# Routing's exponentials ahead of the gelus, route products ahead of an output projection, late normalisations and transposes earlier among the shared experts

## What is computed

```python
x = x + xattn(layernorm(x), ctx, ctx, Wq, Wk, Wv, Wo)   # 16 heads of 8, softmax over the HEADS (axis=1)
x = x + ffn(layernorm(x))

def ffn(x):                       # 8 routed experts, 2 shared ones, F = 512
    raw = x @ centroids.T
    routing_scores = sigmoid(raw); balanced = sigmoid(raw + routing_bias)
    _, top_idx = top_k(balanced, 2)
    top_w = softmax(take(routing_scores, top_idx))
    shared_out = sum over 2 shared experts of gelu(x @ Wfc.T) @ Wproj.T
    routed_out = sum over the 2 chosen experts of top_w * (gelu(x @ Wfc.T) @ Wproj.T)
    return x + shared_out + routed_out
```

## Time and profile before

| | |
|---|---|
| median of three runs | 400.84 us (398.72 to 401.91) |
| the profiled execution | 401.8 us, its span 399.9 us |
| TensorE busy | 319.1 us, 80% of the span |
| VectorE, ScalarE, GpSimd busy | 270.1, 250.5, 258.7 us |
| chain that ended last, by engine | TensorE 31%, issue 24%, VectorE 23%, GpSimd 11% |

### The profile page before, as it was taken

The page is one execution under the profiler, slowest core; times in us unless marked ns, Lnnn a source line. Parts: engine busy times, 40 slices in busy tenths (PEclk is TensorE's granted clock), DMA queues, the critical chain, the costliest instruction groups (busy, mean ns, idle before and its releaser), DMA issues.

```text
span 399.9 us, 11184 instructions
## 1 busy us (share of the span) xinstructions
PE 319.1 (80%) x3828; PEld 258.4 (65%) x3829; DVE 270.1 (68%) x570; ACT 250.5 (63%) x464; POOL 258.7 (65%) x268
## 2 busy tenths in 40 slices
PE   4865786577667687999999999799999999999100
PEld 1562464444444465888788888699898989999100
DVE  3789999989999976652774000367676667676167
ACT  2778798586786762756434355366676776767075
POOL 6344779789787692777777771057777777777500
PEclk9999899988988998999999999999999999999755
DMA  8956343400000000111113612213232232232097
GB/s 255 334 149 246 105 134 112 126 3 2 2 2 2 2 2 7 51 52 55 55 40 96 130 48 75 53 41 88 82 93 83 69 91 74 78 84 62 8 366 259
DMA packets 29176, 36.12 MB, mean 90 GB/s; under 512 B 4932, under 2 KB 24007, under 8 KB 28624
## 3 DMA queue, kind: packets, MB, share of 16 engines
q1 hardware_dynamic: 24592, 27.13, 22.0%
q0 software_dynamic: 4544, 8.44, 6.7%
HBM read 21.74 MB, written 14.72 MB: 91 GB/s over the span
## 4 chain that ended last, share of the span: by engine, by line
PE 31%; issue 24%; DVE 23%; POOL 11%; ACT 5%; DMA 4%; POOLq 1%; SPq 1%; DVEq 1%; ACTq 0%
PE banks L1410 13%; POOL results L502 11%; DVE Z L885 6%; DVE Mx L880 3%; PE banks L1396 3%; PE banks L1395 3%; PE banks L1394 3%; DVE X L1176 2%; DVE rZ L888 1%; ACT E L626 1%; DVE X L1182 1%; DVE stats L856 1%; PE banks L1279 1%; DMA q_rows<-qRep 1%; DMA qRep<-results 1%
## 5 line engine op out<-in xcount | busy, mean ns | idle before, releaser
L502 POOL DMA_INDIRECT results<-E,qRep x78 | 85.9, 1101 | 49.6 <-issue 27.6
L484 POOL DMA_INDIRECT gathered<-xs,slot x64 | 63.4, 991 | 27.6 <-issue 18.6
L430 POOL TENSOR_TENSOR E<-E,rZ 128x1024 f32<-128x1024 f32 x32 | 67.4, 2130 | 18.6 <-DVE rZ L888 18.6
L1147 DVE TENSOR_TENSOR E<-hid,E 128x512 f16<-128x512 f32 x78 | 54.0, 692 | 36.2 <-ACT E L753 36.2
L751 ACT ACTIVATE hid<-banks 128x512 f32<-128x512 f32 x78 | 47.0, 602 | 39.3 <-DVE E L1147 21.8
L1492 PE MATMUL banks<-wprojL,E 128*128 x312 | 54.6, 219 | 2.8 <-DVE E L1147 1.8
L1496 PE MATMUL banks<-wprojH,E 128*128 x312 | 54.3, 219 | 0.0
L1494 PE MATMUL banks<-wprojH,E 128*128 x312 | 54.3, 219 | 0.0
L753 ACT ACTIVATE E<-banks 128x512 f16<-128x512 f32 x78 | 47.3, 606 | 0.0
L626 ACT ACTIVATE E<-banks 128x1024 f32<-128x1024 f32 x32 | 33.2, 1095 | 20.4 <-PE banks L1279 20.4
L1478 PE MATMUL banks<-qRep,wfcH 128*128 128x256 f16 x156 | 42.6, 273 | 0.8 <-ACT E L753 0.6
(11 more groups left out here) (203 smaller groups left out, 726.1 us busy)
## 6 DMA issues: line engine op xcount, KB each, us to landing
qRep<-gathered SPq DMA_DIRECT2D x39, 129.0 KB
qRep<-q_rows SPq DMA_DIRECT2D x32, 128.0 KB, 2.5
qRep<-results SPq DMA_DIRECT2D x8, 512.0 KB, 7.3
X<-in_x SPq DMA_DIRECT2D x4, 512.0 KB, 6.2
q_rows<-qRep SPq DMA_DIRECT2D x8, 256.0 KB, 2.1
out<-X SPq DMA_DIRECT2D x8, 256.0 KB, 4.0
results<-E,qRep POOLq DMA_INDIRECT x78, 2.5
gathered<-spare SPq DMA_DIRECT2D x9, 129.0 KB, 3.9
```

The lines of the kernel that those rows point to most:

```text
L430: g.tensor_tensor(heads, heads, rZ[:, k % 2, :].unsqueeze(1).unsqueeze(3).broadcast_to([P, HH // 2, P, 2]), ALU.mult).then_inc(attn_ready, 1)
L484: g.indirect_dma_start(out=gathered, out_offset=bass.IndirectOffsetOnAxis(ap=slot[:, k, i:i + 1], axis=0), in_=xs[:, i, :], in_offset=None ...
L502: g.indirect_dma_start(out=results, out_offset=bass.IndirectOffsetOnAxis(ap=xg[:, k, h, 2 * D:ROW].bitcast(I32), axis=0), in_=yg[:, k, h, ...
L1147: v.tensor_tensor(gL[:, j, 2 * c:2 * c + 2], hid[:, 2 * j + c].rearrange("p (c q) -> p c q", c=2), gH[:, j, 2 * c:2 * c + 2], ALU.subtract ...
```

## The change

TensorE: the projection of unit 13 moves from ahead of the first up products to behind `route(0)`. Transposes of pair 4 move from behind expert 1 into it (after its second step), those of pair 5 from behind expert 2 to behind expert 1, pair 6 from behind expert 3 to behind expert 2, pair 7 from expert 4 (third step) to expert 3 (second step). `route(1)` moves from behind expert 4 to behind expert 3, `ranks(1)` from the first step of expert 6 to the third step of expert 5. ScalarE: `sigmoid_exps(0)` moves ahead of the four gelus of expert 0 (it stood behind them and behind `copy_o` of unit 14), `copy_o` of unit 14 stands behind the first of these gelus and not the fourth, the normalisations of pairs 4 and 5 stand behind the first and second gelu of expert 1 (both stood ahead of its fourth), the copies of the transposes and `sigmoid_exps(1)` move with TensorE's order. VectorE and GpSimd are untouched, and no instruction is added or taken away but table loads.

```diff
--- before.py
+++ after.py
@@ -706,32 +706,35 @@
                 act.wait_ge(rneed, 2 * portion + 2)
                 s.activation(rt[:, 1:3, lo:hi], rt[:, 1:3, lo:hi], ACT.Exp, scale=-1.0).then_inc(rexp, 1)
 
-            gelus(0, 0, False)
+            sigmoid_exps(0)
+            gelu(0, 0, 0, False)
             act.wait_ge(y_ready, UNITS - 3)
             copy_o(UNITS - 2, 0)
-            sigmoid_exps(0)
+            for c in range(1, FC):
+                gelu(0, 0, c, False)
             act.wait_ge(y_ready, UNITS - 2)
             copy_o(UNITS - 1, 1)
             for c in range(FC):
+                gelu(1, 1, c, False)
+                if c < 2:
+                    second_norm(PAIRS // 2 - 2, c, True)
+            for c in range(FC):
+                if c == 1:
+                    copy_x2(LATE)
                 if c == FC - 1:
-                    for j in range(2):
-                        second_norm(PAIRS // 2 - 2, j, True)
-                gelu(1, 1, c, False)
-            for i in range(2, 4):
-                for c in range(FC):
-                    if c == FC - 1:
-                        copy_x2(LATE + i - 2)
-                    gelu(i, i % 2, c, True)
+                    copy_x2(LATE + 1)
+                gelu(2, 0, c, True)
             for c in range(FC):
                 if c == FC - 1:
                     copy_x2(PAIRS - 2)
-                gelu(4, 0, c, True)
+                gelu(3, 1, c, True)
             for c in range(FC):
-                if c == 2:
+                if c == 1:
                     copy_x2(PAIRS - 1)
                 if c == FC - 1:
                     sigmoid_exps(1)
-                gelu(5, 1, c, True)
+                gelu(4, 0, c, True)
+            gelus(5, 1, True)
             with act.Fori(3, PAIRS - 1) as n:
                 for e in range(2):
                     gelus(2 * n + e, e, True)
@@ -1342,6 +1345,8 @@
                     pe.wait_ge(lo_ready, pair + 1)
                 else:
                     pe.wait_ge(late_ready, pair - LATE + 1)
+                if pair == LATE:
+                    pe.wait_ge(slot_ready, 1)
                 if again:
                     pe.wait_ge(x2_ready, pair)
                 for l in range(2):
@@ -1358,7 +1363,6 @@
             for n in range(2, PAIRS // 2):
                 four_units(n, inputs=True)
             pe.wait_ge(vPad_ready, PAIRS)
-            project_out(UNITS - 3, 1, False)
 
             pe.wait_ge(rstep, 2)
             for part, (lo, hi) in enumerate(WEIGHT_PARTS):
@@ -1395,7 +1399,7 @@
                 t.matmul(up_ps[c], wfcL[:, e, f], x2[:, 0, tok], start=False, stop=False)
                 t.matmul(up_ps[c], wfcH[:, e, f], x2[:, 0, tok], start=False, stop=True).then_inc(up_ready, 1)
 
-            def shared_expert(pair, j, e, i, dn_reused=True, first=False, last=False, ranks_of=None, late_pair=None):
+            def shared_expert(pair, j, e, i, dn_reused=True, first=False, last=False, ranks_at=(), late_pair=None):
 
                 for c in range(FC):
                     if c == 0:
@@ -1411,9 +1415,9 @@
                                                 wproj_shared[e][:, c * D:c * D + D],
                                                 start=(e == 0 and c == 0 and q == 0),
                                                 stop=(e == 1 and c == FC - 1), skip_group_check=True)
-                    if c == 0 and ranks_of is not None:
-                        ranks(ranks_of)
-                    if c == 2 and late_pair:
+                    if ranks_at and c == ranks_at[1]:
+                        ranks(ranks_at[0])
+                    if c == 1 and late_pair:
                         ffn_transposes(late_pair, True)
                 last_product.then_inc(dn_ready, 1)
 
@@ -1421,24 +1425,23 @@
             for c in range(FC):
                 shared_up(0, 0, 0, c, first=True)
             route(0)
+            project_out(UNITS - 3, 1, False)
             for half in range(2):
                 weighted_values(UNITS - 2, 2, half)
             project_out(UNITS - 2, 2, False)
             for half in range(2):
                 weighted_values(UNITS - 1, 3, half)
             project_out(UNITS - 1, 3, False)
-            shared_expert(0, 0, 0, 0, False, first=True, ranks_of=0)
-            shared_expert(0, 0, 1, 1)
-            pe.wait_ge(slot_ready, 1)
-            ffn_transposes(LATE, True)
+            shared_expert(0, 0, 0, 0, False, first=True, ranks_at=(0, 0))
+            shared_expert(0, 0, 1, 1, late_pair=LATE)
+            ffn_transposes(LATE + 1, True)
             shared_expert(1, 1, 0, 2, False)
-            ffn_transposes(LATE + 1, True)
-            shared_expert(1, 1, 1, 3)
             ffn_transposes(PAIRS - 2, True)
-            shared_expert(2, 0, 0, 4, late_pair=PAIRS - 1)
+            shared_expert(1, 1, 1, 3, late_pair=PAIRS - 1)
             route(1)
-            shared_expert(2, 0, 1, 5)
-            shared_expert(3, 1, 0, 6, ranks_of=1)
+            shared_expert(2, 0, 0, 4)
+            shared_expert(2, 0, 1, 5, ranks_at=(1, 2))
+            shared_expert(3, 1, 0, 6)
             shared_expert(3, 1, 1, 7)
             with pe.Fori(2, PAIRS // 2 - 1) as n:
                 for j in range(2):
```

## The result

The changed kernel takes 403.39 us (median of 20 runs, 401.88 to 405.86) against 401.10 us (20 runs): ratio 1.006, 95% interval 1.0045 to 1.0075, so about 2.4 us slower. The forecast was 404.4 us in a range of 400.3 to 407.5. The profiled execution has a span of 400.4 us, only 0.5 above the one of before. The following lines show why both are true.

The account below looks back on a forecast made before the run. TensorE was taken as fully busy from 157.2 us, so delays before it, waiting for the route's decision, count. +3.85 + 0.76 + 0 - 0.96 = +3.65, say +3.6, on the median of 400.84: 404.4 us, range 400.3 to 407.5.

Parts of the forecast that it names:

- low stretch behind `ranks`: TensorE after `ranks`: low clock again loses 1.6 us as before, so 0 in the sum; bounds 0 and twice 1.6.
- The chain through ScalarE's order: First portion: exponentials, table load and gelu delay unit 14's copy, projection, addition and the choice of experts: +3.85 us.
- rival 2: VectorE's L971 not held by GpSimd, scores ready at 144.5, 1.95 us earlier: +1.7 us, 402.5; chance 0.19.
- The route products earlier give nothing: Route products end 2.26 us earlier on TensorE, but GpSimd still holds VectorE's copy and bias addition: 0, bounds 0 and 1.95.
- The low clock on the projection: Unit 14's projection on TensorE runs at the low clock after idle time: +0.76 us, bounds 0 and 0.76.
- the first rival: Clock recovers in time, so TensorE runs at full clock after `ranks`: +2.0 us, 402.8; chance 0.18.
- shared experts' end at 257 to 258: Sign of the forecast: TensorE finishes the shared experts at 257 to 258 us.
- The late part: Moved normalisations and transposes cause no wait (0); earlier second routing removes TensorE's stall at pair 3 (-0.96 us); loads at 247.5.
- The two table loads that go give nothing: Two of ScalarE's three table loads in the first portion go, 1.28 us each, both hidden before: 0.

Follow-up runs that it names:

- The edit alone: The kernel before with only ScalarE's first-portion order changed (exponentials, first gelu, copy of unit 14, three gelus, copy of unit 15): ratio 1.0078.
- its undoing: The changed kernel with ScalarE's first-portion exponentials put back behind the four gelus and the copy of unit 14: 399.70 us, ratio 0.9974.
- PSUM run: The changed kernel with the scores' copy and bias addition reading the route's products straight from PSUM: 399.51 us, ratio 0.9962.
- filled kernel: The changed kernel with 27 idle products of 512 columns on TensorE ahead of unit 14's projection: 403.30 us, ratio 1.0067.
- late part alone: The kernel before with only the changed order of normalisations, transposes, their copies, second route and its ranks: 400.07 us, ratio 0.9977.
- scores first: The changed kernel with scores from PSUM ahead of unit 13's addition, unit 14's copy before all gelus, its addition inside the choice: 395.73 us, ratio 0.9881.

## Why the prediction was right, and where it was off

The direction, the mechanism and the place of the loss were right, and 403.39 us lies well inside the range of 400.3 to 407.5. The size was too large: +3.6 us was forecast, and the interval of the measurement is +1.8 to +3.0 us. One term of the sum, the low stretch behind `ranks`, makes that difference.

*The chain through ScalarE's order*: right in mechanism and size. The steps were a copy of unit 14 behind exponentials, one table load and one gelu, then the projection, then the choice. Counted from GpSimd's first multiplication, the copy was forecast at 10.85 and came at 10.80, the choice's first step 13.66 (at low clock) and 13.68, `ranks` 19.3 and 19.33. (The chain from the first step to `member` has fourteen steps, not sixteen; its 5.68 us were measured as a whole and came back as 5.65.) In absolute time `ranks` stood at 155.79, which read by itself would have spoken for rival 2 ("near 155"); only the count from the common event shows the forecast's place. The edit alone and its undoing show it from both sides (+4.59 and -4.61 us at `ranks`).

*The route products earlier give nothing*: right. The copy L974 was held 1.30 us, to GpSimd's third boundary (136.46 + 3 x 2.10 = 142.76), and the bias addition began behind the start of the fourth and took 2.22 us. That removed the second rival. The two kernels that differ in this part alone (400.07 and 399.70 us) fit that. The Trainium skill (SBUF — State Buffer, section Who interferes with whom) says that VectorE in a two-port mode, or with two SBUF inputs, contends with GpSimd, and that with at most one SBUF input outside these modes it doesn't. It names `copy` among the instructions that can take such a mode, so the prediction misread it where it says that by this page L971, a copy from SBUF to SBUF, would pass. The trace of the changed kernel and the PSUM run agree with the page: 1.30 and 2.22 us from SBUF against 0.29 and 0.28 us from PSUM.

*The low clock on the projection* (+0.76): right, 2.08 us and not 1.16, so +0.92. Filling the idle time took it away (1.16 us in two traces).

*The low stretch again behind `ranks`* (1.6 taken, bounds 0 and 3.2): this is the term that was mis-sized. It measured 0: in both profiles of the changed kernel the low stretch spans 6.8 us of the idle time and the projection, and is over by 151.3 or 152.4. With it at 0 the sum is +2.0, and measured are +1.92 at the routed experts and +2.4 in time. That is the first rival, which had 0.18 of the chances against the forecast's 0.45; its +2.0 lies inside the interval of the measurement, the forecast's +3.6 doesn't.

The sign "shared experts' end at 257 to 258" failed with this term: TensorE's first product of the routed experts is at 255.06, or 256.5 when counted from GpSimd's multiplication as in the kernel before.

The term was taken from the likeness to the kernel before, thin use ahead of `ranks`. There TensorE idled 2.98 us ahead of it, here 1.61, and the filled kernel shows that the stretch can return (2.38 us idle ahead of `ranks`, low clock behind it). But the late part alone idled 2.54 us there and ran at full clock behind it, after a low stretch that ended 11 us earlier. So the idle time just ahead of `ranks` doesn't decide it alone, and what does isn't shown.

*The late part*: right. TensorE is busy in all 32.80 us from 157.2 and all 4.00 from 190.0, the stall is gone, and the part alone gives 0.9977 (with 1 at the edge of its interval). SyncE's loads are at 246.03, 9 us ahead of their use; counted from GpSimd's multiplication that is 109.57, where 109.6 (247.5) had been worked out.

*The two table loads that go give nothing*: no run shows this by itself. What speaks for it are idle times of ScalarE: behind the load at 144.74 in the kernel before it idled 0.47 us for the bias, so that load held up nothing.

The absolute time of the forecast, 404.4, rested on one profiled execution and a median of three runs; over 20 the kernel before is 401.10, and from there the forecast would have been 404.7 and the first rival 403.1.

## What to carry to other kernels

Moving an operation ahead on one engine moves everything behind it back: before putting a wait early, ask what small copy stands behind it and whose chain it feeds. A saving before a held instruction is worth nothing until the hold is removed; where VectorE works while GpSimd multiplies, where its operand lies is part of its cost (1.30 and 2.22 us from SBUF, 0.29 and 0.28 from PSUM here). And judge an order by several executions or from a common event, since one profile can differ by more than the effect for reasons ahead of the change.

## What the hardware showed that was not expected

- A low-clock stretch is not only a price but has a place: where TensorE idles anyway it costs nothing, on a full engine 1.6 us. With 6.0 us of the idle time filled by products there was none in that place, in two traces, and one came behind `ranks`, where it cost more. Its length differs too, 3.4 us or 6.8: the kernel with the bias from PSUM had 6.8 in one set and 3.4 in the other.
- A VectorE instruction that waited for GpSimd got through between two back-to-back GpSimd instructions without lengthening them (8.40 us for four, with the copy waiting in the changed kernel and without it in the PSUM kernel; 8.47 in scores first), but the next one, 1.23 us behind it, was held for the whole of the fourth.
- A VectorE operation with one SBUF input (`tensor_scalar`, float32, 128x256, in place) was held too, 2.09 us and not 0.29.
